# Factors of heads 2 and 3 from TensorE sums, output bias on one tile of y, and a new order of VectorE and the DMA queue in the first heads

## The reference, cut to what matters

```python
x = x + _layernorm(_L0_attn_ref(_layernorm(x), Wq, bq, Wk, bk, Wv, bv, Wo, bo, gq, gk))
x = x + _layernorm(_L0_ffn_ref(_layernorm(x), ...))

# in _L0_attn_ref, INNER = 32 * 128
q = rms_norm(h @ Wq + bq, gq)      # the mean square runs over all 4096 columns
k = rms_norm(h @ Wk + bk, gk)
v = h @ Wv + bv
attn = softmax(q @ k.T / sqrt(128))        # per head
out = (attn @ v) over all heads @ Wo + bo
```

## Time and profile before

| what | value |
|---|---|
| median of 3 runs | 1121.79 us (1121.17 to 1123.26) |
| the profiled execution | 1119.13 us |
| its span, first to last instruction | 1117.3 us |
| PE busy | 1067.6 us, 96% |
| DVE busy | 803.4 us, 72% |
| ACT busy | 728.6 us, 65% |
| POOL busy | 675.3 us, 60% |
| mean granted clock of PE | 0.984 of 2.4 GHz |

### The profile page before, as it was taken

One profiled execution on the slowest core, in us unless ns is written; L12 is line 12 of the kernel. 1 busy time (PEld: TensorE's weight loads), 2 busy tenths in 40 slices (PEclk: granted clock), 3 DMA queues, 4 the chain that ended last, 5 costly groups with the idle time before them and its releaser, 6 DMA issues.

```text
span 1117.3 us, 19743 instructions
## 1 busy us (share of the span) xinstructions
PE 1067.6 (96%) x5720; PEld 579.0 (52%) x5720; DVE 803.4 (72%) x1799; ACT 728.6 (65%) x1427; POOL 675.3 (60%) x537
## 2 busy tenths in 40 slices
PE   6869999999999989999999999999999999999896
PEld 3324444444444545555555555555555555555385
DVE  7666666676675467777777777777777777777886
ACT  4456666666665566777777777776676777776532
POOL 2446676666666556666666676676676666664423
PEclk9989999999999889999999999999999999999999
DMA  7695665665563289576676666667667666666602
GB/s 267 178 250 199 233 218 199 221 221 208 210 181 95 102 227 225 156 196 179 161 194 171 168 189 174 169 182 182 168 176 188 169 175 182 170 165 155 164 1 75
DMA packets 313220, 199.50 MB, mean 179 GB/s; under 512 B 275680, under 2 KB 279904, under 8 KB 313056
## 3 DMA queue, kind: packets, MB, share of 16 engines
q1 hardware_dynamic: 313184, 199.07, 62.2%
HBM read 96.24 MB, written 35.68 MB: 118 GB/s over the span
## 4 chain that ended last, share of the span: by engine, by line
PE 60%; issue 19%; POOL 13%; DVE 4%; ACT 2%; DMA 1%; SPq 1%; POOLq 0%; DVEq 0%
PE ps L1072 20%; PE ps L1073 20%; PE ps L1074 20%; POOL acc L589 8%; POOL qk_out L571 3%; DVE stats L1384 1%; POOL acc L620 1%; ACT ps L908 1%; DVE y L1822 1%; DMA qk_in<-x 0%; DVE ps L1752 0%; DVE y L1735 0%; PE ps L1158 0%; DMA y<-x 0%; SPq L533 0%
## 5 line engine op out<-in xcount | busy, mean ns | idle before, releaser
L1752 DVE TENSOR_SCALAR_CACHE_REDUCE ps<-ps,score_down 128x512 f32<-128x512 f32 x256 | 177.5, 755 | 97.1 <-PE ps L1074 96.7
L1766 DVE SCALAR_TENSOR_TENSOR pair_q<-ps,row_inv,pair_q 128x512 f16<-128x512 f32 x256 | 174.5, 744 | 61.1 <-ACT pair_q L917 59.9
L1072 PE MATMUL ps<-xh,wa_hi 128*128 128x512 f16 x512 | 196.2, 383 | 16.9 <-DVE qk_out L1589 14.6
L908 ACT ACTIVATE ps<-ps,neg_max 128x512 f32<-128x512 f32 x256 | 168.0, 656 | 47.2 <-DVE ps L1752 47.2
L1073 PE MATMUL ps<-xl,wa_hi 128*128 128x512 f16 x512 | 196.1, 383 | 0.0
L1074 PE MATMUL ps<-xh,wa_lo 128*128 128x512 f16 x512 | 195.7, 382 | 0.0
L664 POOL CAST oth<-o_t 128x512 f16<-128x512 f32 x62 | 37.9, 611 | 217.1 <-ACT o_t L893 217.1
L917 ACT ACTIVATE pair_q<-ps,row_inv 128x512 f16<-128x512 f32 x256 | 155.1, 688 | 21.1 <-DVE row_inv L1759 21.1
L571 POOL TENSOR_TENSOR qk_out<-q_s,qk_out 128x512 f16<-128x512 f32 x64 | 73.9, 1157 | 123.1 <-ACT qk_out L791 123.1
L589 POOL TENSOR_TENSOR acc<-acc,squares 128x1024 f32<-128x1024 f32 x60 | 140.4, 2360 | 0.0
L1073 PE MATMUL ps<-wv_lo,xh 128*128 128x256 f16 x512 | 139.6, 273 | 0.0
(11 more groups left out here) (181 smaller groups left out, 2238.1 us busy)
## 6 DMA issues: line engine op xcount, KB each, us to landing
q_k_scratch<-qk_out SPq DMA_DIRECT2D x64, 512.0 KB, 3.4
qk_in<-q_k_scratch SPq DMA_DIRECT2D x64, 512.0 KB, 3.3
wa_stage<-w_qk SPq DMA_DIRECT2D x32, 512.0 KB, 3.9
u_stage<-w_vo SPq DMA_DIRECT2D x32, 512.0 KB, 4.9
wv_stage<-w_vo SPq DMA_DIRECT2D x16, 512.0 KB, 4.5
wo_stage<-w_vo SPq DMA_DIRECT2D x16, 512.0 KB, 4.2
qk_tops<-qk_top_scratch SPq DMA_DIRECT2D x30, 128.0 KB, 4.5
y<-x SPq DMA_DIRECT2D x8, 256.0 KB, 4.9
```

The source lines that it names most:

```text
L908: act.activation(ps[:, SCORE + i, :], ps[:, SCORE + i, :], ACT.Exp, bias=neg_max[:, sl, i:i + 1], scale=-1.0, accum_out=row_sum[:, sl, i:i ...
L1072: pe.matmul(outp, lhs[0], rhs[0], start=first, stop=False)
L1752: dve.tensor_scalar(ps[:, SCORE + i, :], ps[:, SCORE + i, :], score_down[:, sl, i:i + 1], None, ALU.mult, ALU.min, accum_out=neg_max[:, sl ...
L1766: dve.scalar_tensor_tensor(out=pair_q[:, 1, i, :], in0=ps[:, SCORE + i, :], scalar=row_inv[:, sl, i:i + 1], in1=pair_q[:, 0, i, :], op0=AL ...
```

## The change

Heads 2 and 3 get their factors as heads 0 and 1 do: `largest_sums(2)` and `(3)` on TensorE, at positions 4 and 6, into banks 7 and 1 (table `SUMS`), and `first_factors(2)` and `(3)` on VectorE, which then also make the columns. TensorE gets three waits with it: position 6 waits for head 0's first key to be stored, position 7 and the first looped head for the sums to have been read. In the loop TensorE's one pair of waits ahead of a head is spread: its first item waits for the query's low half and for `k_out_ready` at 2h − 3, its second for the key's low half, its third for 2h − 1. The stores and loads of the tops of heads 2 and 3 are gone, and the counts of the later ones are lower by two. Only the last tile of `y` is loaded with `bo`; when pair 0's rows are added, each tile reads that tile as its second operand, the last one in place. The first loads of `wv_stage` and `wo_stage` move from the start-up to just ahead of the queue's loop. The orders of VectorE and of the queue in heads 0 and 1 are new.

```diff
+        SUMS = (5, 5, 7, 1)
...
             load_wa(3, 3)
-            sp.dma_start(wv_stage..., w_vo[0]).then_inc(wv_loaded, 16)
-            sp.dma_start(wo_stage..., w_vo[PAIRS]).then_inc(wo_loaded, 16)
...
             def load_tops(h, par):
-                sp.wait_ge(qk_top_stored, 16 * (h - 1))
+                sp.wait_ge(qk_top_stored, 16 * (h - 3))
...
             load_wa(5, 1)
-            store_tops(2, 0)
-            load_tops(2, 0)
-            store_tops(3, 1)
-            load_unit(2, 0, 2)
-            load_unit(3, 1, 3)
-            load_tops(3, 1)
             sp.wait_ge(x_turned, NT)
-            for t in range(NT):
-                sp.dma_start(y[:, t, :], bo).then_inc(y_set, 16)
+            sp.dma_start(y[:, NT - 1, :], bo).then_inc(y_set, 16)
             store_qk(0, 0, 0, 1)
-            store_qk(1, 1, 0, 2)
             sp.wait_ge(wa_lo_ready, 6)
             load_wa(6, 2)
+            load_unit(2, 0, 2)
             store_tops(4, 0)
+            store_qk(1, 1, 0, 2)
+            store_qk(0, 0, 1, 3)
+            load_unit(3, 1, 3)
             load_tops(4, 0)
-            store_qk(0, 0, 1, 3)
             store_tops(5, 1)
+            store_qk(1, 1, 1, 4)
             load_unit(4, 0, 4)
-            store_qk(1, 1, 1, 4)
+            sp.dma_start(wv_stage..., w_vo[0]).then_inc(wv_loaded, 16)
+            sp.dma_start(wo_stage..., w_vo[PAIRS]).then_inc(wo_loaded, 16)
...
             def largest_sums(h):
-                pe.matmul(ps[:, 5, 2 * h:2 * h + 2], ones[:, :], qk_top[:, h, :],
+                pe.matmul(ps[:, SUMS[h], 2 * h:2 * h + 2], ones[:, :], qk_top[:, h % 2, :],
...
                 if pos == 4:
                     pe.wait_ge(xl_ready, NT)
+                    largest_sums(2)
+                if pos == 6:
+                    pe.wait_ge(k_out_ready, 1)
+                    largest_sums(3)
+                if pos == 7:
+                    pe.wait_ge(qk_down_ready, 6)
                 q_or_k(par, g, par)
...
             def phase_a(i, o):
+                pe.wait_ge(wa_lo_ready, 2 * h + 1)
+                pe.sem_inc(pe_begun, 1)
+                pe.wait_ge(k_out_ready, 2 * h - 3)
+                q_or_k(par, 0, o % 4)
                 pe.wait_ge(wa_lo_ready, 2 * h + 2)
-                pe.sem_inc(pe_begun, 1)
+                q_or_k(par, 1, o % 4)
                 pe.wait_ge(k_out_ready, 2 * h - 1)
-                for g in range(4):
-                    q_or_k(par, g, o % 4)
+                q_or_k(par, 2, o % 4)
+                q_or_k(par, 3, o % 4)
+            pe.wait_ge(qk_down_ready, 8)
...
             def first_factors(h):
                 for w in range(2):
-                    dve.tensor_scalar(qk_down[:, h, w:w + 1], ps[:, 5, ...], LEAST, 1.0 / W_UP, ...)
+                    least = least_q[:, h:h + 1] if h >= 2 and w == 0 else LEAST
+                    dve.tensor_scalar(qk_down[:, h, w:w + 1], ps[:, SUMS[h], ...], least, 1.0 / W_UP, ...)
                 dve.sem_inc(qk_most_ready, 1)
                 inverses_up(h, h)
+                if h >= 2:
+                    query_bias(h, h)
+                    key_columns(h, h)
...
             dve.wait_ge(k_cols_ready, 6)
+            first_factors(2)
+            largest_qk(3, 1, 3, 16)
             store_k(0, 0, 0, 2)
             largest_of_unit(0, 0, 16)
-            largest_qk(3, 1, 3, 16)
+            low_wa(2, 2)
+            first_factors(3)
+            largest_qk(4, 0, 0, 32)
+            store_k(1, 0, 1, 4)
             largest_of_unit(1, 1, 16)
-            store_k(1, 0, 1, 4)
-            next_factors(2, 0, 2)
-            largest_qk(4, 0, 0, 32)
-            low_wa(2, 2)
+            store_k(0, 1, 0, 6)
+            low_wa(3, 3)
+            largest_qk(5, 1, 1, 32)
             largest_of_unit(2, 0, 32)
-            store_k(0, 1, 0, 6)
-            next_factors(3, 1, 3)
-            largest_qk(5, 1, 1, 32)
-            low_wa(3, 3)
+            store_k(1, 1, 1, 8)
             largest_of_unit(3, 1, 32)
-            store_k(1, 1, 1, 8)
...
-            def add_y(count, tile, bank):
+            def add_y(count, tile, bank, to=None):
+                to = tile if to is None else to
                 return dve.scalar_tensor_tensor(out=y[:, tile, :], in0=ps[:, bank, :], scalar=y_down[:, :],
-                                                in1=y[:, tile, :], op0=ALU.mult, op1=ALU.add)
+                                                in1=y[:, to, :], op0=ALU.mult, op1=ALU.add)
...
-            dve.wait_ge(y_set, 16 * NT)
+            dve.wait_ge(y_set, 16)
             for s in range(4):
-                step(1, s, 1)
+                step(1, s, 1, to=NT - 1)
```

More of the change, by code:

```diff
@@ L372, in _ @@
             load_wa(3, 3)
-            sp.dma_start(wv_stage[:, :, :].rearrange("p c n -> p (c n)"), w_vo[0]).then_inc(wv_loaded, 16)
-            sp.dma_start(wo_stage[:, :, :].rearrange("p h n -> p (h n)"), w_vo[PAIRS]).then_inc(wo_loaded, 16)
             for u in range(2):
@@ L424, in _ @@
             load_wa(5, 1)
-            store_tops(2, 0)
-            load_tops(2, 0)
-            store_tops(3, 1)
-            load_unit(2, 0, 2)
-            load_unit(3, 1, 3)
-            load_tops(3, 1)
             sp.wait_ge(x_turned, NT)
-            for t in range(NT):
-                sp.dma_start(y[:, t, :], bo).then_inc(y_set, 16)
+            sp.dma_start(y[:, NT - 1, :], bo).then_inc(y_set, 16)
             store_qk(0, 0, 0, 1)
-            store_qk(1, 1, 0, 2)
             sp.wait_ge(wa_lo_ready, 6)
             load_wa(6, 2)
+            load_unit(2, 0, 2)
             store_tops(4, 0)
+            store_qk(1, 1, 0, 2)
+            store_qk(0, 0, 1, 3)
+            load_unit(3, 1, 3)
             load_tops(4, 0)
-            store_qk(0, 0, 1, 3)
             store_tops(5, 1)
+            store_qk(1, 1, 1, 4)
             load_unit(4, 0, 4)
-            store_qk(1, 1, 1, 4)
+            sp.dma_start(wv_stage[:, :, :].rearrange("p c n -> p (c n)"), w_vo[0]).then_inc(wv_loaded, 16)
+            sp.dma_start(wo_stage[:, :, :].rearrange("p h n -> p (h n)"), w_vo[PAIRS]).then_inc(wo_loaded, 16)
             with sp.Fori(1, PAIRS // 2 - 1) as i:
@@ L1461, in first_factors @@
                 for w in range(2):
-                    dve.tensor_scalar(qk_down[:, h, w:w + 1], ps[:, 5, 2 * h + w:2 * h + w + 1], LEAST, 1.0 / W_UP,
-                                      ALU.max, ALU.mult).then_inc(qk_down_ready, 1)
+                    least = least_q[:, h:h + 1] if h >= 2 and w == 0 else LEAST
+                    dve.tensor_scalar(qk_down[:, h, w:w + 1], ps[:, SUMS[h], 2 * h + w:2 * h + w + 1], least,
+                                      1.0 / W_UP, ALU.max, ALU.mult).then_inc(qk_down_ready, 1)
                 dve.sem_inc(qk_most_ready, 1)
                 inverses_up(h, h)
+                if h >= 2:
+                    query_bias(h, h)
+                    key_columns(h, h)
             def next_factors(h, par, slot):
-                dve.wait_ge(qk_tops_loaded, 16 * (h - 1))
+                dve.wait_ge(qk_tops_loaded, 16 * (h - 3))
                 dve.tensor_reduce(qk_most[:, slot, :], qk_tops[:, par].rearrange("p q w -> p w q"), AX.X,
@@ L1769, in low_halves, with add_rows, step @@
                                          op1=ALU.subtract).then_inc(low_ready, 1)
-            def add_rows(s, n):
+            def add_rows(s, n, to=None):
                 for k in range(2):
-                    add_y(2 * n - 5 + k, 2 * ((s + 1) % 4) + k, YB + k).then_inc(y_added, 1)
-            def step(p, s, par, first=False, value=True, rows=True, down=True, bank=VB):
+                    add_y(2 * n - 5 + k, 2 * ((s + 1) % 4) + k, YB + k, to).then_inc(y_added, 1)
+            def step(p, s, par, first=False, value=True, rows=True, down=True, bank=VB, to=None):
                 n = 4 * p + s
@@ L1782, in step @@
                 if rows:
-                    add_rows((s - 1) % 4, n - 1)
+                    add_rows((s - 1) % 4, n - 1, to)
                 inverses(n, sl)
```

## The result

| | before | changed |
|---|---|---|
| first comparison, median of four runs each | 1121.48 us | 1104.44 us (1102.6 to 1106.31), ratio 0.985 [0.983, 0.987] |
| repeated on a second chip | 1120.84 us | 1107.75 us (1106.62 to 1111.13), ratio 0.988 [0.986, 0.990] |
| repeated on a third chip | 1118.85 us | 1106.88 us (1105.02 to 1108.06), ratio 0.988 [0.987, 0.990] |

The change is 17 us faster in the first comparison and 12 to 13 us in the other two. The profiled execution took 1106.31 us with a span of 1104.3, the slowest of the first four, so the two profiles differ by only 13.0 us of span.

A forecast was written before the change was run, and what follows sets the result against it. TensorE bounds the first phase, so its idle before 69 us delays everything. Holes 14.4, tails 0.3 and slow restart 1.75 make 16.45 us, less 0.3 for the sums: 16.1 off 1121.79 gives 1105.7 us, range 1103.0 to 1111.5.

The forecast's parts named there:

- hole one: TensorE's idle 2.50 us before 42.70 us, ended by VectorE's late `store_k`; predicted to be gone.
- hole two: TensorE's idle 11.87 us before 65.11 us, from head 4's memory round trip behind other transfers; predicted gone, narrowly.
- the slow restart: Nine TensorE matmuls from 65.11 us took 3.69 us instead of 1.94; 1.75 us to be saved.
- The sums: Two `largest_sums` added on TensorE, taken at 0.15 us each, 0.3 in all; bounds 0 and 0.6.
- VectorE's new order: VectorE from 30.6 us: head 3's factors done at 37.4, key (0,1) at 41.4, unit 3 at 47.2.
- Head 4's round trip: Largest weights stored at 38.7, landed 43.8, loaded 48.3; head 2's first key at 54.9, needed 55.9: slack 1.0 us.
- Head 5 on: Head 5's load leaves near 49, VectorE asks at 57.5; slack grows by over 1 us a head.
- rival A: Head 4's memory round trip still ends last, a 3.7 us hole; about 1110 us, up to 1111.1; chance 0.27.
- The bias loads as the cause: TensorE's stall before 65.11 us was laid to a memory round trip behind 2 MB of `bo` and other transfers.
- Rival B: Two more TensorE waits per looped head, not hidden, make it slower; 1123.9 us at 0.65 a head; chance 0.03.
- C: No gain: TensorE stops for head 4's memory trip as long as before; 1121.8 us; chance 0.03.
- 1 MB of `wv` and `wo`: These loads leave the start-up, where no TensorE wait hangs on them, and are issued near 46 us.

The follow-up runs named there:

- E1: The kernel before with one edit, output bias loaded on the last tile of `y` alone, one load in place of eight; 1115.3 us, ratio 0.997.
- E5: The kernel before with heads 2 and 3 getting their factors from TensorE's sums, all else as before; 1116.6 us, ratio 0.997.
- E9: The changed kernel with the old order of the queue in heads 0 and 1; 1110.45 us, ratio 0.993.
- E4: The changed kernel with TensorE's waits of a looped head all ahead of its first item, as before; 1112.59 us, ratio 0.995.
- E3: The changed kernel with the first `wv` and `wo` loads back at the start-up; 1103.64 us, ratio 0.986; again 1103.12 us.
- E6: The changed kernel with the first `wv` and `wo` loads right behind the load of head 5's weights; 1106.11 us, ratio 0.986.
- E2: The changed kernel with all eight bias loads at the place of the one; 1107.77 us, ratio 0.990.
- the repeat: The changed kernel itself, unedited, measured again on the second chip; 1107.75 us, ratio 0.988.

## Why the prediction was right

The forecast was 1105.7 us, a saving of 16.1 from TensorE running on through heads 0 to 3; measured were 1104.44, 1107.75 and 1106.88, savings of 17.0, 13.1 and 12.0. The range held all three. What the change removes, hole one, hole two and the slow restart, is the prediction's mechanism as it stood. That the first median came within 1.3 us of the forecast is in part luck: the traces account for a saving of 13 us, and the sum left out what heads 4 and 5 gave back.

- *Hole one, hole two, the slow restart*, 16.45 us: all three gone, as the windows and the timeline show. TensorE's first looped head followed the eighth item without a gap.
- *The sums*: 0.14 us each (the next matmul starts 0.14 after them), 0.15 taken.
- *VectorE's new order*: the factor set of head 3 was done at 38.07, key (0,1) ended at 41.84, expected 37.4 and 41.4; the start-up was 0.87 late in that execution. Right within 0.5 us up to there.
- *Head 4's round trip*: store 39.30 (38.7), landed by 45.12, so 5.8 (5.1), and taken up at 49.50 (48.3). Head 2's first key was stored at 56.06 (54.9), TensorE wanted it at about 56.7 (55.9): slack 0.7 of the 1.0 given. All four are, within 0.3 us, the forecast's numbers plus the late start. The 49.50 is so in part by chance: VectorE, which the forecast had free at 47.2, was itself busy until then, because of `low_wa(3)`.
- *Head 5 on*: this is the step that was wrong. I had the load leave near 49, land about 54 and be wanted at 57.5; it left at 52.66 and was taken up at 61.84. Two terms were mis-sized. The 1.4 us of `low_wa(3)` came from a row where GpSimd was idle; beside GpSimd's sums it took 3.5, so that key (1,1) ended at 48.2 and not at 46.0, and the six transfers behind it left from 48.3. And the queue was counted at 0.42 MB/us from the moment of issue, where the 128 KB broadcast took 9.2 us from issue to use. The sentence that the slack grows by over 1 us a head is right for VectorE, but the memory trips of heads 5 and 6 did not keep to it. So 1.6, 2.2 and 4.6 us were given back at heads 4 and 5 in the three traces. It is rival A's mechanism one head further on; I had looked for it at head 4 only.
- *The bias loads as the cause*: the prediction gave hole two to "2 MB of `bo` and other transfers" and leaned on the first. E1 shows 4.5 of the 11.9 us to be theirs. The rest hung on what else stood ahead, which a single edit does not free (E1, E5, E9).
- *Rival B* (extra waits) and *C* (nothing): refuted by E4 and by the result.
- *1 MB of `wv` and `wo` "near 46, ahead of head 5's"* was seen and waved through on the estimate above; E3 prices it at some 2 to 4 us.
- *The signs*: the holes of hole one and two were gone and the store left near 38.7, as listed. Two signs failed, a wait on `qk_tops` under 1.5 us (it was 3.29) and a window that is full and 16 us earlier (257.42 of 259.00, and 13 us).
- *The lower end*: 1121.79 less 16.45 less 2 is 1103.3, not 1103.0. Nothing hangs on it.

What stays open: why the saving was 17 us once and 12 to 13 twice. The slower DMA engines in the second chip's trace (share 0.72 against 0.63) go with larger holes there, but the third chip's trace had 0.64, with 2.2 us at heads 4 and 5 and 1.64 before the last head. And the holes of the first phase are not the whole of it: in the second chip's trace that phase ended 6.1 us later than in the first, the span only 2.5. The start-up varied by up to 2 us between executions (the turn of tiles 4 to 7 from 24.97 to 27.07 us); its cause was not tried.

## What to carry to other kernels

A small store that another engine waits for pays for everything issued before it on its queue, so list what stands ahead of it, and what each of those issues itself waits for; an edit that frees only one of them may gain a quarter of what all together do. When a slack of 1 us decides, do the same sum for the next two trips as well, with durations from rows where the neighbouring engines are as busy as they will be then. A load with no deadline, moved next to such a trip, can cost more than in its own place in the start-up; an idle stretch of the queue just before the trips was not clearly better (E6). And look for the same trip elsewhere in the kernel: here one before the last head cost up to 2.7 us and was left alone.

## What the runs showed of the hardware

- **VectorE beside GpSimd.** A pair of `scalar_tensor_tensor` with two SBUF inputs took 1.41 us with GpSimd idle and 3.51 while GpSimd added squares. GpSimd in the changed kernel's trace:

```profile
38.48 4.67 POOL L586 TENSOR_TENSOR acc<-acc,squares 128x1024 f32<-128x1024 f32 x2
43.11 1.61 POOL L568 TENSOR_TENSOR qk_out<-q_s,qk_out 128x512 f16<-128x512 f32 x1
```

  Its `low_q`, 1.16 us alone, took 1.61 there, so both lose. The single instructions of that stretch:

```profile
40.80 2.35 POOL L586 TENSOR_TENSOR acc<-acc,squares 128x1024 f32<-128x1024 f32 x1
41.75 1.95 DVE L1500 SCALAR_TENSOR_TENSOR wa_lo<-wa_stage,qk_up,wa_hi 128x512 f16<-128x512 f32 x1
43.62 1.64 DVE L1500 SCALAR_TENSOR_TENSOR wa_lo<-wa_stage,qk_up,wa_hi 128x512 f16<-128x512 f32 x1
44.68 2.80 POOL L586 TENSOR_TENSOR acc<-acc,squares 128x1024 f32<-128x1024 f32 x1
```

  VectorE's first ended 0.55 us after GpSimd's addition, its second 0.54 us after GpSimd's `low_q` (43.11 to 44.72), and the next addition took 2.80 instead of 2.33: they went by turns. The extra 2.1 us are two such waits, of about 1.2 and 0.9. The Trainium skill ("SBUF — State Buffer", section "Who interferes with whom") says that a VectorE instruction with two SBUF inputs contends with a GpSimd instruction that reads SBUF, and that the shared pair of ports is an exclusive lock. The trace agrees. VectorE's reductions and PSUM reads in the same stretch kept their 1.21 and 0.80 us.
- **The clock after a short hole.** Holes of 2.50 (before) and 2.61 us (E1) left it high, and after 3.79, 5.57, 7.40, 9.62 and 11.87 the first matmul was at the 1.2 GHz level. The 3.79 us (E4) settle what rival A had left open for its 3.7. But after 2.22 (E6), 2.50 (E2), 2.72 (E5) and 2.82 us (the repeat) PE started fast and fell to that level 0.2 to 0.9 us later, for some eight matmuls, which is 1.7 us; and after 2.26 (E6) and 2.54 (the repeat, 345.13 above) already the first matmul was slow. So a hole of 2 to 3 us can cost nearly twice its length, and the same hole may not.
- **A bulk load in an idle queue.** Eight loads of 256 KB with the first query store moved at 0.29 MB/us on average (E2), against 0.42 in the earlier trace rows. Single slices reached 0.41, and issuing the eight took 5.1 us, so the average does not say that the DMA engines themselves were slower.
- **The time to landing.** 1 KB landed 3.1 us after its issue at the least and 9.8 at the most in the kernel before, up to 110 us, and 9.4 us behind 2.8 MB in E1; the broadcast of 128 KB took 4.4 us for head 4 and 9.2 for head 5 in the changed kernel.
